# A sixteen-layer network on one core: expert slots of 128 tokens, and an attention core whose TensorE follows a written plan

## Time and profile before

| | us |
|---|---|
| three runs | 6273.28, 6275.22, 6287.34; median 6275.22 |
| profiled execution, its own time | 6273.15 |
| its span, first to last instruction | 6271.4 |

### The profile page before, as it was taken

One profiled execution on the slowest core, in us unless ns is written; L12 is line 12 of the kernel. 1 busy time (PEld: TensorE's weight loads), 2 busy tenths in 40 slices (PEclk: granted clock), 3 DMA queues, 4 the chain that ended last, 5 costly groups with the idle time before them and its releaser, 6 DMA issues. The chain is left out here.

```text
span 6271.4 us, 90519 instructions
## 1 busy us (share of the span) xinstructions
PE 4874.7 (78%) x33371; PEld 2083.9 (33%) x33466; DVE 3773.5 (60%) x4700; ACT 3169.5 (51%) x5938; POOL 1644.0 (26%) x1264
## 2 busy tenths in 40 slices
PE   5777658886678866688765887849976799688799
PEld 2232223332222235222253222326532244222244
DVE  6899546764677732778424876277738710578510
ACT  5665336665456732367512776534456521477621
POOL 0666137672211124311153111000005500311100
PEclk8999869998889988899986999969988999799999
DMA  0000031110312123321133111000000000101100
GB/s 25 0 1 0 4 101 31 38 36 18 95 34 46 36 62 98 107 45 40 41 99 119 34 41 42 8 10 2 2 13 0 19 0 1 59 23 40 40 0 14
DMA packets 150368, 222.90 MB, mean 36 GB/s; under 512 B 44966, under 2 KB 74514, under 8 KB 148564
## 3 DMA queue, kind: packets, MB, share of 16 engines
q1 hardware_dynamic: 144084, 209.16, 12.2%
q0 software_dynamic: 5888, 8.43, 0.4%
HBM read 137.92 MB, written 81.23 MB: 35 GB/s over the span
## 5 line engine op out<-in xcount | busy, mean ns | idle before, releaser
L914 ACT ACTIVATE l_core_probs<-l_core_ps_scores_b 128x512 f32<-128x512 f32 (+3 forms) x3840 | 1612.7, 500 | 983.7 <-PE l_core_ps_scores_b L826 780.1
L985 DVE TENSOR_REDUCE l_core_chunk_max<-l_core_ps_scores_a 128x2 f32<-128x1024 f32 (+3 forms) x1280 | 1272.1, 1022 | 344.4 <-PE l_core_ps_scores_a L807 180.2
L826 PE MATMUL l_core_ps_scores_b<-l_q_rows_sb,l_k_rows_sb 64*128 64x512 bf16 (+3 forms) x3840 | 943.5, 338 | 265.0 <-ACT l_core_probs L914 222.4
L807 PE MATMUL l_core_ps_scores_a<-l_k_rows_sb,l_q_rows_sb 64*128 64x512 bf16 (+3 forms) x3840 | 763.0, 346 | 252.4 <-DVE l_core_chunk_max L985 148.2
L942 POOL TENSOR_SCALAR_AFFINE_SELECT l_core_probs<-l_core_probs 128x512 f32<-128x512 f32 x512 | 327.3, 639 | 1804.8 <-ACT l_core_probs L914 1804.8
L826 PEld LDWEIGHTS l_core_ps_scores_b<-l_q_rows_sb,l_k_rows_sb 64*128 64x128 bf16 x3840 | 274.4, 94 | 1167.0 <-ACT l_core_probs L914 955.3
L845 PE MATMUL l_core_ps_acc<-l_core_probs,l_v 128*9 128x512 f32 (+3 forms) x6144 | 659.5, 502 | 0.0
L985 DVE TENSOR_REDUCE l_core_neg_max<-l_core_ps_scores_a 128x2 f32<-128x256 f32 (+3 forms) x640 | 504.5, 821 | 82.6 <-PE l_core_ps_scores_a L768 80.8
L1858 POOL TENSOR_TENSOR l_scan_bx<-l_xs,l_scan_b_rows 128x1024 f32<-128x1024 f32 x192 | 452.5, 2357 | 224.1 <-DVE l_scan_states L1868 217.8
L1868 DVE TENSOR_TENSOR_SCAN l_scan_states<-l_scan_ps_decay,l_scan_bx 128x1024 f32<-128x1024 f32 x192 | 439.8, 2290 | 40.7 <-POOL l_scan_bx L1858 15.3
L933 POOL TENSOR_TENSOR l_core_probs_decayed<-l_core_probs,l_decay 128x1536 f32<-128x1536 f32 (+2 forms) x160 | 392.0, 2476 | 218.0 <-ACT l_core_probs L914 217.9
(11 more groups left out here) (316 smaller groups left out, 7391.2 us busy)
## 6 DMA issues: line engine op xcount, KB each, us to landing
l_q_rows<-l_proj_parts SPq DMA_DIRECT2D x96, 256.0 KB, 5.7
l_k_rows<-l_proj_parts SPq DMA_DIRECT2D x96, 256.0 KB, 5.1
l_q_rows_sb<-l_q_rows SPq DMA_DIRECT2D x128, 192.0 KB
l_k_rows_sb<-l_k_rows SPq DMA_DIRECT2D x128, 192.0 KB
l_slots_weights<-m_both_dram SPq DMA_DIRECT2D x46, 512.0 KB
l_heads_out<-l_core_out_sums SPq DMA_DIRECT2D x300, 32.0 KB
l_q_rows_sb<-l_core_max_parts SPq DMA_DIRECT2D x480, 4.0 KB, 1.8
l_core_heads<-l_heads_out SPq DMA_DIRECT2D x15, 512.0 KB, 5.5
```

Source lines behind the costliest of these rows:

```text
L807: mm = nc.tensor.matmul(slot[:, i, 0:w], qs[n % 3][rows, p, qt * P:(qt + 1) * P], ks[n % 3][rows, p, c * NT:c * NT + w], start=True, stop= ...
L826: mm = nc.tensor.matmul(pb[(m + i) % 3][:, 0:w], ks[n % 3][rows, p, kt * P:(kt + 1) * P], qs[n % 3][rows, p, q0:q0 + w], start=True, stop= ...
L914: nc.scalar.activation(pt[:, ts % RP, j, 0:w], pb[m % 3][:, 0:w], ACT.Exp, scale=scale).then_inc(b_free, 1)
L985: nc.vector.tensor_reduce(to, pa[e % 2][:, :, 0:width_a(qt, c)], AX.X, ALU.max, negate=True).then_inc(a_free, 1)
```

## The change

**Projection.** SP stores only q; ACT stores k, after its second rounding step of the following sequence. Without rotation, DVE makes the third part, three pieces behind its values, and POOL only subtracts once.

**Attention core.** PE follows a string per group, one letter per piece of work: `a` a query-major unit, `b` one key-major product, `v` a values product. There are 48 b, 12 v and 25 a in each string, one for the plain cores, one for the core with decay, whose lag grows to 3 and whose probabilities have 5 buffers in place of 4. Masks are issued half by half. The row maxima are copied by 3 DMAs of two rows each. The reciprocals of the first three sequences stand before unit 20 in place of 12; that of the last sequence stands behind the sixth output unit. Four output units move into group 14 (`EARLY`), three further late units stand at a-letters 2, 4 and 17 of group 15 (`LAST_AT`), the rest at the end.

**Experts.** Slots of 128 rows: (4096-8)/128 = 31, plus 8, gives 39 slots, one gather and one scatter each. Gathered rows have 8 buffers, weights 8, results 4, up products 4; a scatter stands six slots behind its gather, the down product two slots behind the up product. The constants of the routing follow the new size.

```diff
+PLAN = ("babbvb", "bababbav", "bbabavba", "bbvbb", "bababab", "bvbabvb",
+        "bababvab", "bbavbba", "bvbbabaa", "bbaabvb", "bbaavabb", "bvbabb")
+PLAN_DECAY = ("bbbvbaa", "bbvbba", "bvbabba", "babbb", "bbabavbaa", "bbvabba",
+              "bvbabbav", "bbabvab", "bbvabba", "bavbbbaav", "bbabab", "bvbbbaa")
...
 def attn_project(...):
-                    for j, n in enumerate("qk"):
-                        for slot in range(6):
-                            sp.dma_start(parts[n].rearrange("(b h s d) t -> b s h d t", b=B, s=6, d=dq)[b, slot],
-                                         part[0:R, j, PAIRS[slot][j], b * S:(b + 1) * S]
-                                         ).then_inc(stored if b else first_stored, 16)
+                    for slot in range(6):
+                        sp.dma_start(parts["q"].rearrange("(b h s d) t -> b s h d t", b=B, s=6, d=dq)[b, slot],
+                                     part[0:R, 0, PAIRS[slot][0], b * S:(b + 1) * S]
+                                     ).then_inc(stored if b else first_stored, 16)
...
+                def plain_third(n):
+                    h, j = n // 2 % 2, n % 2
+                    tok = slice(n // 2 * NT, (n // 2 + 1) * NT)
+                    dve.wait_ge(mid, n + 1)
+                    nc.vector.tensor_tensor(part[0:R, j, 2, tok], t1[0:R, j, h, :], part[0:R, j, 1, tok],
+                                            ALU.subtract).then_inc(low, 1)
...
+                    for n in range(4 * B):
+                        plain_value(n)
+                        if n >= 3:
+                            plain_third(n - 3)
...
+                def store_k(b):
+                    act.wait_ge(low, 4 * b + 4)
+                    for slot in range(6):
+                        act.dma_start(parts["k"].rearrange("(b h s d) t -> b s h d t", b=B, s=6, d=dq)[b, slot],
+                                      part[0:R, 1, PAIRS[slot][1], b * S:(b + 1) * S]
+                                      ).then_inc(stored if b else first_stored, 16)
...
+                for b in range(B):
                     for m in range(4):
                         first(b, m)
                         if m:
                             second(b, m - 1)
+                        if b and m == 1:
+                            store_k(b - 1)
                     second(b, 3)
+                store_k(B - 1)
...
 def attn_core(...):
-    LAG, RP, RW = 2, 4, 3
+    LAG, RP, RW = (3, 5, 3) if decay else (2, 4, 3)
...
+    EARLY, LAST_AT = 4, (2, 4, 17)
...
-        MIN = 16 * 6
+        MIN = 16 * 3
...
-                    for i in range(2):
-                        for e in range(3):
-                            row = 64 * i + r0 + e
-                            sp.dma_start(qs[u][row:row + 1, :, :].rearrange("o p (k q) -> o (p k) q", q=P),
-                                         mpart[16 * i:16 * i + 16, e, :]).then_inc(m_in, 16)
+                    for e in range(3):
+                        sp.dma_start(qs[u][r0 + e:r0 + e + 65:64, :, :].rearrange("i p (k q) -> i (p k) q", q=P),
+                                     mpart[:, e, :]).then_inc(m_in, 16)
...
+                def unit_b(n, t, j):
                     c, kt = STEPS[t]
                     w, q0 = width_b(c, kt), first_q(c, kt)
+                    m, p, i = 4 * (NS_ * n + t) + j, j // 2, j % 2
                     diag = decay and q0 == kt * P
+                    if m >= 3:
+                        pe.wait_ge(b_free, m - 2)
+                    rows = slice(64 * i, 64 * i + 64)
+                    mm = nc.tensor.matmul(pb[m % 3][:, 0:w], ks[n % 3][rows, p, kt * P:(kt + 1) * P],
+                                          qs[n % 3][rows, p, q0:q0 + w], start=True, stop=not diag)
                     if diag:
+                        mm = masked(pb[m % 3][:, 0:P], i, maskk, (slice(0, 64), slice(0, P)))
+                    mm.then_inc(b_ready, 1)
...
+                    for kind in "".join(PLAN_DECAY if decay else PLAN):
+                        if kind == "a":
+                            if n < GROUPS - 1 and e < DONE_A[GROUPS - 1] + EARLY or n == GROUPS - 1 and a in LAST_AT:
                                 unit_a(e)
+                                e += 1
+                            a += 1
+                        elif kind == "b":
+                            unit_b(n, b // 4, b % 4)
+                            b += 1
+                        else:
+                            if v_at >= 0:
+                                values(v_at)
+                            v_at += 1
...
-                    if t + 2 < TILES:
+                    if t < EARLY:
                         scale_heads(t + 2)
+                    if t == 5:
+                        invert(B - 1, 12)
+                        scale_heads(6)
+                        scale_heads(7)
...
-                    if n in (6, 10, 14) and k == NA // 2:
+                    if n in (6, 10, 14) and k == NA - 4:
                         invert(n // 4 - 1, HEADS)
...
-                        invert(B - 1, 12)
...
-SLOT = 2 * P
+SLOT = P
...
 def experts_slots(...):
-    XR, YR, WR = 4, 3, 3
-    AHEAD = 3
+    XR, YR, WR = 8, 4, 8
+    AHEAD = 6
...
-        pu = ps("up", [P, 2, HC, SLOT])
+        px = [ps(f"turned_x{n}", [P, NT]) for n in range(2)]
+        pu = ps("up", [P, 4, HC, SLOT])
...
-                for j in range(SLOTS + 1):
+                for j in range(SLOTS + 2):
                     if j + 1 < SLOTS:
                         turn_in(j + 1)
                     if j < SLOTS:
                         up(j)
-                    if j >= 1:
-                        down(j - 1)
+                    if j >= 2:
+                        down(j - 2)
```

217 lines of the change are left out of this document (93 added, 124 removed).

## The result

The changed kernel takes **5782.7 us** (median of 4 runs, 5776.8 to 5786.4) where the kernel before, run beside it, takes 6276.6: a ratio of **0.921, interval 0.9194 to 0.9225**. 5788 was predicted, and 5680 to 5960. The profiled execution took 5786.37 (span 5784.7), 486.7 us less span than before. The total is close; the parts are less so.

What follows compares the result with a forecast made beforehand. No engine was taken as full; the order of work set the core's pace. Plain cores -302, decay core -56, slots -108 and projections -21 gave -487 us from 6273.15, so 5786, and 5788 as median; range 5680 to 5960.

Steps and rivals of the forecast that it cites:

- Plain group: Plain attention cores: single issue and interleaved values bring a group from 28.6 to 25.5 us, bounds 24.0 and 28.6.
- rival (c): Attention cores: DVE's floor is reached, 24.0 us a group, 30.2 in decay, total 5681 us; chance 0.14.
- Decay group: Layer 2's core: a group falls from 33.8 to 31.3 us, PE's 30.2 plus 1.1 of wait; bounds 30.2 and 34.5.
- Reciprocals: Three groups per core: moved eight units later, the reciprocal's 2.2 us wait goes and its 0.95 us stay.
- Last group and tail: End of each plain core: 34 us against 47.7, so -13.5, with units moved into group 14 costing nothing there.
- Masks: Attention cores: masks ordered by half cost PE at most 1.3 us more a group; taken as nothing.
- Row maxima: Attention cores: three DMAs in place of six issue 1.8 us earlier, exposed only at group 0: -1 us a core.
- Slots: Expert stages: 103 us of GpSimd against 121, a stage 125 us against 179, -54 each; GpSimd over 80% busy.
- Projections: Five projections: layer 14 -14 us, layers 2 and 8 -3.5 each, rotating layers nothing; sum -21, bounds 0 and -45.
- (a): Attention cores: PE becomes the bound as singly issued products each pay, 27.8 us a group, total 5958 us; chance 0.22.
- (b): Expert slots: stay bound elsewhere, by late gathers or weights, both stages at 165 us, total 5868 us; chance 0.10.
- (d): Attention cores: query-major units stand behind single products waiting for ACT, about 35 us a group, total 6576 us; chance 0.02.

Runs made afterwards that it cites:

- experiment 4: The changed kernel, one part undone per layer: middle reciprocals, core +9.0 us; six maxima DMAs, 452.4; interleaved masks, 439.5; late units, +2.7; decay's two-step lag and four buffers, 571.5.
- experiment 3: The changed kernel with other TensorE orders per layer: values at step's end 28.7 us a group, pairs 26.3, both 29.3 to 30.8, previous planner's order 28.6 (layer 8), decay 33.5.
- experiment 2: The changed kernel with all projection stores back on SyncE, the new division of subtractions kept: 5767.9 us, ratio 0.9202.

## Why the prediction was right, and where it was not

**Plain group: right mechanism, mis-sized term.** "I take 0.4 for all: 12 x 0.4 = 4.8 us" of ACT's waiting, 25.5 us a group. ACT waits 4.0, and the group takes 24.5, between the forecast and rival (c)'s 24.0. The term that was mis-sized gave every values product the cost of one that stands between two b with nothing in hand; the timeline above has one standing where three exponentials are still to be done. DVE is idle for only 1.4 us of the group, so it is nearer to being full than ACT. Over 60 groups that 1 us is more than the plain cores' extra gain of 38 us; group 14 takes part of it back. **Decay group**: 30.1 where 31.3 was taken. The lower bound of 30.2 was TensorE's busy time of before, and that fell too, to 28.4. The lag and the fifth buffer, given one sentence and no price, are worth 2.7 us a group (experiment 4).

**Reciprocals**: the waits went, as predicted, and only 0.4 of the 0.95 us stayed. **Last group and tail**: 32.4 against 34, from 47.7. But "they cost PE some 4 us but stand after all of that group's query-major units", so nothing, was wrong: group 14 takes 4.8 us more than a plain group and 5.7 to 6.3 more than without them. Experiment 4 shows that the placing of the late units and of the last reciprocal is worth 2.7 us net of that. The two stretches together took 78.6 us in layer 14 before and take 62.3 now; with the planner's order in the new kernel (layer 8 of experiment 3) they take 71.0, so about half of this came with the even order. The 8.4 us behind the last exponential are 8.25 by the earlier trace rows, which changes nothing. **Masks**: nothing, as taken.

**Row maxima**: taken at -1 and "exposed only at group 0". That was read from groups of 28.6 us. At 24.5 the three DMAs are worth 11 us a core (experiment 4): a cost taken as hidden, whose cover the same change removed. From the Trainium skill's rule on the number of engines (DMA: Bandwidth & Descriptors, on why a DMA increments its semaphore by 16), two for a DMA of two rows, the prediction concluded that they land later. If so, by little: the group begins 2.6 us behind the last issue. How many engines one used, no run here shows.

**Slots**: 103 us of GpSimd, 13.3 us of tail, 129.1 and 124.1 against 125. Right, by its own steps; only the sign "GpSimd over 80% busy" failed as worded (66%), as the issue gaps of the 103 us are not counted as busy. The runs add that look-ahead and weight buffers brought more (32 us) than the slot size (18 to 23).

**Projections: the failed step.** "Rotating layers: nothing, as compute and DMA volume stay, the cover being the full DMA engines", and for layer 14 that SyncE would shed 15 us of issues. Volume did stay, but the issues moved onto the engine in the middle of the chain of roundings (DVE, ACT, GpSimd, ACT), where six of them hold it for up to 7.46 us, 1.24 each. The parts come later, and the last store with them: +9.0 and +9.6 us, not 0. Layer 14's -14 failed by a second step, that issues handed over are issues saved. Its 3.6 us are about what the six issues take that ACT makes while SyncE loads stacks (3.9 us from 4973.53). For the rest both issue at once, and SyncE's 18 remaining q stores take 17.3 us, 0.96 each, not 0.64. The computing did shed time, 10.8 us to the last rounding with all stores on SyncE (experiment 2), but it did not set the end. The Trainium skill (DMA: Bandwidth & Descriptors, Issuing engines are not separate DMA queues) says that a second issuer saves only issue time. In layer 14 the trace shows less than that where both issue at once (0.59 us an issue against 0.64, last section), and in the rotating layers the second issuer pays the time itself.

**Rivals.** (a) PE bound did not come: PE has 23.8 us in 24.5 and the "bb" letters still overlap. It is nonetheless 97% busy by the profile, so that "wrong if PE is over 95% busy" was a poor sign without its second half, 27 us. (b) and (d) did not come. (c) came in part for the plain group, with 24.5 between 25.5 and 24.0. For the decay group its number came to 0.1 us, but not as a floor: in the 30.1 us PE is busy 28.4 and DVE 26.7. That the total came within 6 us is luck: the errors have opposite signs, cores 51 us better, projections 37 worse, other stages 12 worse.

## What to carry to other kernels

Where an engine feeds another through a few buffers, look at what the feeder does between two refills: the same work with its long pieces put right behind a refill made the group 4 us of 28 shorter, and the piece's place counted more than how singly the refills are issued. A DMA issued from a compute engine is work on that engine; put it on one whose next instruction nobody waits for. After every gain ask again what was hidden only because the stage was slow, and count look-ahead as distance between stages, not as number of buffers.
